# An AdaLN-conditioned FFN on one Trainium2 core: prologue order, six rows spread by DMA, borrowed buffers moved

## What is computed

```
att   = softmax(gelu(gelu(emb W0 + b0) W1 + b1) W2 + b2)          # 32 x 8, emb = cond_128
y[b]  = (sum_k att[b,k] weight[k]) x[b] + (att bias_k)[b]         # 128x128 by 128x2048, "conv"
yb    = bfloat16(y)
qg,sg = dynamic_quant(yb * inv_gate);  qu,su = dynamic_quant(yb * inv_up)   # codes -127..127, a scale a row
gate  = (qg w_gate^T) sg s_gate;       up = (qu w_up^T) su s_up            # 2048 -> 1024
inter = bfloat16(clip(silu(gate) up, -10, 10))
qi,si = dynamic_quant(inter * inv_inter)
out   = x + (qi w_down^T) si s_down                                # 1024 -> 2048
```

## Time and profile before

| | |
|---|---|
| median of the runs | 838.83 us (838.81 to 840.03) |
| profiled execution, its own time | 838.61 us |
| its span, first to last instruction | 836.8 us |
| PE busy | 811.7 us, 97% |
| DVE, ACT, GpSimd busy | 715.6, 443.0, 152.1 us |
| bytes moved by DMA | 117.72 MB |
| mean granted TensorE clock | 0.993 |

### The profile page before, as it was taken

The page is one execution under the profiler, slowest core; times in us unless marked ns, Lnnn a source line. Parts: engine busy times, 40 slices in busy tenths (PEclk is TensorE's granted clock), DMA queues, the critical chain, the costliest instruction groups (busy, mean ns, idle before and its releaser), DMA issues.

```text
span 836.8 us, 9194 instructions
## 1 busy us (share of the span) xinstructions
PE 811.7 (97%) x3531; PEld 365.9 (44%) x3531; DVE 715.6 (86%) x799; ACT 443.0 (53%) x379; POOL 152.1 (18%) x146
## 2 busy tenths in 40 slices
PE   7898969899999999999999999999999999999997
PEld 2344434344444444444444444444444444444443
DVE  5575847999888898888889988888898888889968
ACT  2767322566565555565555556555555565545541
POOL 5630002111222222012222210222221012222000
PEclk9999989999999999999999999999999999999999
DMA  9962534355445454444554544445454454554242
GB/s 272 216 149 51 101 101 169 104 159 160 113 151 164 139 164 139 117 140 120 164 160 142 141 136 139 113 151 163 139 162 141 119 132 127 164 157 145 89 113 101
DMA packets 157918, 117.72 MB, mean 141 GB/s; under 512 B 147497, under 2 KB 147625, under 8 KB 148274
## 3 DMA queue, kind: packets, MB, share of 16 engines
q1 hardware_dynamic: 156146, 104.55, 41.4%
q0 software_dynamic: 1728, 12.58, 7.5%
HBM read 59.44 MB, written 33.55 MB: 111 GB/s over the span
## 4 chain that ended last, share of the span: by engine, by line
PE 88%; DVE 6%; ACT 2%; DMA 2%; issue 1%; DVEq 0%; ACTq 0%
PE up_ps L506 24%; PE gate_ps L506 24%; PE down_ps L580 24%; PE conv_ps L453 13%; DVE amax L875 1%; DMA wd<-w_downT 1%; DMA qgT<-qg 1%; PE down_ps L423 1%; DVE region L965 1%; DVE region L971 1%; ACT qg L686 0%; PE up_ps L423 0%; DVE region L981 0%; PE gate_ps L580 0%; PE conv_ps L415 0%
## 5 line engine op out<-in xcount | busy, mean ns | idle before, releaser
L506 PE MATMUL gate_ps<-wg,qgT 128*128 128x512 bf16 x992 | 219.7, 379 | 1.6 <-ACT qgT L730 1.6
L580 PE MATMUL down_ps<-wd,qiT 128*128 128x512 bf16 x912 | 214.8, 379 | 2.1 <-ACT qiT L766 2.1
L506 PE MATMUL up_ps<-wu,quT 128*128 128x512 bf16 x960 | 216.7, 379 | 0.0
L875 DVE TENSOR_REDUCE amax<-region 128x1 f32<-128x2048 f32 (+1 forms) x93 | 178.8, 1923 | 1.3
L357 POOL TENSOR_TENSOR prod<-wexp,att_bc 128x1024 f32<-128x1024 f32 x31 | 58.9, 1901 | 541.6 <-DVE region L915 516.6
L506 PEld LDWEIGHTS gate_ps<-wg,qgT 128*128 128x128 bf16 x992 | 96.9, 98 | 119.4 <-ACT qgT L730 2.1
L580 PEld LDWEIGHTS down_ps<-wd,qiT 128*128 128x128 bf16 x912 | 89.1, 98 | 128.0 <-issue 30.0
L506 PEld LDWEIGHTS up_ps<-wu,quT 128*128 128x128 bf16 x960 | 93.8, 98 | 113.5 <-issue 0.6
L453 PE MATMUL conv_ps<-xt,aggw 128*128 128x512 f32 x256 | 124.7, 612 | 6.1 <-issue 2.9
L686 ACT ACTIVATE qg<-region,recip 128x2048 f16<-128x2048 f32 x30 | 60.1, 2002 | 125.9 <-DVE recip L885 125.9
L677 ACT ACTIVATE y<-conv_ps,aggb 128x512 bf16<-128x512 f32 x120 | 81.8, 686 | 75.4 <-PE conv_ps L453 70.7
(11 more groups left out here) (124 smaller groups left out, 509.3 us busy)
## 6 DMA issues: line engine op xcount, KB each, us to landing
xt<-x SPq DMA_DIRECT2D x32, 1024.0 KB, 4.8
out<-xt SPq DMA_DIRECT2D x31, 1024.0 KB, 4.0
wg<-w_gateT POOLq DMA_DIRECT2D x4, 1024.0 KB, 19.0
wu<-w_upT POOLq DMA_DIRECT2D x4, 1024.0 KB, 19.5
wd<-w_downT POOLq DMA_DIRECT2D x4, 1024.0 KB, 7.7
out<-xt SPq DMA_DIRECT2D x4, 256.0 KB, 2.7
wexp<-weightT SPq DMA_DIRECT2D x1, 512.0 KB, 3.8
qgT<-qg SPq DMA_TRANSPOSE x28, 3.7
```

What stands on the lines that cost most here:

```text
L506: last = nc.tensor.matmul(acc[:, n * BANK:(n + 1) * BANK], codes[:, k * P:(k + 1) * P], wts[:, k, n * BANK:(n + 1) * BANK], start=(k == 0) ...
L580: last = nc.tensor.matmul(down_bank(t, c), qiT_at(t)[:, k * P:(k + 1) * P], wd[:, k, c * BANK:(c + 1) * BANK], start=(k == 0), stop=(k == ...
L875: nc.vector.tensor_reduce(amax[:, i:i + 1], src, axis=AX.X, op=ALU.max, apply_absolute_value=True).then_inc(max_ready, 1)
```

## The change

- The six rows are arrays of their own. SyncE spreads each over all partitions by one DMA (`partition_broadcast(P)`), inv_gate behind x tile 0, inv_up and s_gate once w_gate's third quarter is in (`sp.wait_ge(wg_in[2], 16)`), s_up, inv_inter and s_down once its last is in. x tile 3 is sent behind them.
- PE's spread and warm products, ACT's spread_copy and GpSimd's partition_broadcast go. Those who waited for spread_out or row_spread wait for rows_in of the row.
- GpSimd's aggregate(1) waits for agg_step K, the end of aggregate(0) on DVE, instead of att_dve 7.
- GATE_HOME[1] is `prod` instead of part 5 of `wd`; QIT_HOME is in `qg` instead of `prod`. So gate_out(1) on DVE waits for agg_ready 4, turned_i(0) on ACT for the turning of qg(3) on PE, quant_g(4) on ACT for down_done 8, and GpSimd no longer waits for down_done 8 ahead of aggregate(5). Other waits that served the old homes go.
- Order on PE: turn_u(0) ahead of gate(2, h0) instead of behind it. On ACT: quant_g(1) ahead of conv_out(2); turned_g(2), quant_u(0), turned_u(0) and then silu(0); quant_g(3) ahead of silu(2); quant_u(3) behind turned_i(2). On DVE: quant_g(3) ahead of gate_out(2), and quant_u(3) behind inner(2).

The diff, cut to its core:

```diff
-        GATE_HOME = [down_sc2[:, :], wd_part(5, fp32), wd_part(6, fp32)]
+        GATE_HOME = [down_sc2[:, :], prod[:, :, :].rearrange("p k o -> p (k o)"), wd_part(6, fp32)]
...
-        prod_bf = prod[:, :, :].rearrange("p k o -> p (k o)").bitcast(bf16)
-        QIT_HOME = [prod_bf[:, 0:KI * P], prod_bf[:, KI * P:2 * KI * P]]
+        qg_bf = qg[:, :].bitcast(bf16)
+        QIT_HOME = [qg_bf[:, 0:KI * P], qg_bf[:, KI * P:2 * KI * P]]
...
 @block.sync
             sp.dma_start(mlp_s, mlp).then_inc(mlp_in, 16)
             sp.dma_start(b2_s, b2.partition_broadcast(P)).then_inc(b2_in, 16)
-            sp.dma_start(invg_s[0], rows[:, 0:I]).then_inc(rows_in[0], 16)
             sp.dma_start(wexp[:, :, :], weightT).then_inc(wexp_in, 16)
-            sp.dma_start(invg_s[1], rows[:, I:2 * I]).then_inc(rows_in[1], 16)
             sp.dma_start(xslot(0), x[0, :, :]).then_inc(x_in[0], 16)
+            sp.dma_start(invg_bc[:, :], inv_gate.partition_broadcast(P)).then_inc(rows_in[INVG], 16)
             sp.dma_start(xslot(1), x[1, :, :]).then_inc(x_in[1], 16)
-            for i, home in enumerate((invu_s[0], invu_s[1], swg_s)):
-                sp.dma_start(home, rows[:, (2 + i) * I:(3 + i) * I]).then_inc(rows_in[2 + i], 16)
             sp.dma_start(xslot(2), x[2, :, :]).then_inc(x_in[2], 16)
-            for i, home in enumerate((swu_s, invi_s, swd_s[0], swd_s[1])):
-                sp.dma_start(home, late_rows[:, i * I:(i + 1) * I]).then_inc(late_in[i], 16)
+            sp.wait_ge(wg_in[2], 16)
+            sp.dma_start(invu_bc[:, :], inv_up.partition_broadcast(P)).then_inc(rows_in[INVU], 16)
+            sp.dma_start(swg_bc[:, :], s_gate.partition_broadcast(P)).then_inc(rows_in[SWG], 16)
+            sp.wait_ge(wg_in[3], 16)
+            sp.dma_start(swu_bc[:, :], s_up.partition_broadcast(P)).then_inc(rows_in[SWU], 16)
+            sp.dma_start(invi_bc[:, :], inv_inter.partition_broadcast(P)).then_inc(rows_in[INVI], 16)
+            sp.dma_start(swd_bc[:, :], s_down.partition_broadcast(P)).then_inc(rows_in[SWD], 16)
             sp.wait_ge(gcodes_ready, 2)
             sp.dma_start(xslot(3), x[3, :, :]).then_inc(x_in[3], 16)
...
 @block.gpsimd
-            pool.wait_ge(att_dve, ATT - 1)
+            pool.wait_ge(agg_step, K)
             aggregate(1)
...
-            for i in range(4):
-                pool.wait_ge(late_in[i], 16)
-            spread(swu_bc[:, :], swu_s)
-            spread(invi_bc[:, :], invi_s)
-            spread(swd_bc[:, 0:I], swd_s[0])
-            spread(swd_bc[:, I:H], swd_s[1])
...
-            pool.wait_ge(row_spread, SWD)
             load(wd, w_downT, 2, wd_in)
             pool.wait_ge(prod_ready, 3)
             load(wd, w_downT, 3, wd_in)
-            pool.wait_ge(down_done, NC * 2)
...
 @block.tensor
-            pe.wait_ge(ones_set, 1)
-            warm(9)
             pe.wait_ge(mlp_in, 16)
+            pe.wait_ge(ones_set, 1)
             nc.tensor.matmul(hid_ps, w0_s, embT_s, start=True, stop=True).then_inc(hid_mm, 1)
-            warm(1)
...
-            warm(3)
...
-            for u in range(4):
-                spread(u)
-                warm(1)
             conv(0)
-            spread(4)
-            spread(5)
             conv(1)
             turn_g(0)
             conv(2)
             gate(0, HALVES[0])
-            spread(6)
-            spread(7)
             turn_g(1)
             gate(0, HALVES[1])
-            spread(8)
-            spread(9)
             gate(1, HALVES[0])
             turn_g(2)
             gate(1, HALVES[1])
+            turn_u(0)
             gate(2, HALVES[0])
-            turn_u(0)
             conv(3)
...
 @block.scalar, quant_g(t)
+                elif t == EARLY + 1:
+                    act.wait_ge(down_done, NC * 2)
 turned_u(t)
-                if t == 1:
-                    act.wait_ge(row_spread, SWD)
 turned_i(t)
                 if t == 0:
-                    act.wait_ge(agg_ready, 4)
+                    act.wait_ge(gturn_mm, GTURN["g", EARLY] + 2)
 order
-            for u in range(4):
-                spread_copy(u)
             conv_out(0)
-            spread_copy(4)
-            spread_copy(5)
             conv_out(1)
             quant_g_first()
             turned_g(0)
+            quant_g(1)
             conv_out(2)
-            quant_g(1)
-            spread_copy(6)
-            spread_copy(7)
             turned_g(1)
             quant_g(2)
-            spread_copy(8)
-            spread_copy(9)
+            turned_g(2)
             quant_u(0)
-            turned_g(2)
+            turned_u(0)
             silu(0)
-            turned_u(0)
             quant_u(1)
             conv_out(3)
             silu(1)
             turned_u(1)
             quant_u(2)
+            quant_g(3)
             silu(2)
-            quant_g(3)
             turned_u(2)
             quant_i(0)
-            quant_u(3)
             turned_g(3)
             turned_i(0)
             quant_i(1)
             turned_i(1)
             quant_i(2)
             turned_i(2)
+            quant_u(3)
             turned_u(3)
...
 @block.vector, gate_out(t)
-                if t == 2:
-                    dve.wait_ge(row_spread, SWD)
+                if t == 1:
+                    dve.wait_ge(agg_ready, 4)
 order
             quant_u(2)
+            quant_g(3)
             gate_out(2)
-            quant_g(3)
             inner(0)
-            quant_u(3)
             inner(1)
             inner(2)
+            quant_u(3)
```

More of the change, by code:

```diff
@@ L3, with adaln_ffn @@
 from contextlib import ExitStack
-def adaln_ffn(nc, x, mlp, b2, weightT, w_gateT, w_upT, w_downT, rows, late_rows, out):
+def adaln_ffn(nc, x, mlp, b2, weightT, w_gateT, w_upT, w_downT, inv_gate, inv_up, s_gate, s_up, inv_inter, s_down, out):
     fp32 = mybir.dt.float32
@@ L168, in adaln_ffn @@
         wexp_in = sem("wexp_in")
-        rows_in = [sem(f"rows_in{i}") for i in range(5)]
-        late_in = [sem(f"late_in{i}") for i in range(4)]
+        rows_in = [sem(f"rows_in{i}") for i in range(6)]
         x_in = [sem(f"x_in{i}") for i in range(XS)]
@@ L237, in adaln_ffn @@
         result_ready = sem("result_ready")
-        INVG, INVU, SWG = 4, 8, 10
-        SWU, INVI, SWD = 1, 2, 4
+        INVG, INVU, SWG, SWU, INVI, SWD = range(6)
         ATT = 8
@@ L250, in adaln_ffn @@
         last_turn_ps = [bank(up_ps, h).bitcast(fp16)[:, 0:BANK] for h in range(2)]
[L252 to L257, removed]
         def gate_acc(t):
@@ L365, in aggregate @@
                 nc.gpsimd.tensor_tensor(w, prod[:, 0, :], prod[:, 1, :], ALU.add).then_inc(agg_ready, 1)
-            def spread(dst, row):
-                nc.gpsimd.partition_broadcast(dst, row).then_inc(row_spread, 1)
             nc.gpsimd.memset(ident[:, :], 0.0).then_inc(ident_set, 1)
@@ L411, in _ @@
         def _(pe):
[L413 to L424, removed]
+            pe.wait_ge(mlp_in, 16)
             pe.wait_ge(ones_set, 1)
-            warm(9)
-            pe.wait_ge(mlp_in, 16)
             nc.tensor.matmul(hid_ps, w0_s, embT_s, start=True, stop=True).then_inc(hid_mm, 1)
-            warm(1)
             pe.wait_ge(hid_act, 1)
             nc.tensor.matmul(hid_ps, w1_s, h1, start=True, stop=True).then_inc(hid_mm, 1)
-            warm(3)
             pe.wait_ge(att_dve, 1)
@@ L444, in conv @@
                 for c in cs:
-                    if t == 0 and c < 2:
-                        pe.wait_ge(spread_out, 3)
-                    elif t == 3 and c < 2:
+                    if t == 3 and c < 2:
                         pe.wait_ge(uturn_out, c + 1)
@@ L450, in conv @@
                         pe.wait_ge(uturn_out, 9 + c)
-                    else:
+                    elif t > 0 or c >= 2:
                         pe.wait_ge(y_ready, NC * t + c - 1)
@@ L513, in gate @@
                         pe.wait_ge(qgT_ready, t - EARLY)
-                    if t == 0:
-                        pe.wait_ge(spread_out, INVG)
-                    elif t == 1:
-                        pe.wait_ge(spread_out, SWG)
-                    elif t == 2:
+                    if t == 2:
                         pe.wait_ge(gateval_ready, 1)
@@ L521, in gate @@
                         pe.wait_ge(upval_ready, 2)
-                    else:
+                    elif t > EARLY:
                         pe.wait_ge(gateval_ready, t)
@@ L659, in _ @@
         def _(act):
-            def spread_copy(u):
-                act.wait_ge(spread_mm, u + 1)
-                nc.scalar.activation(SPREAD_INTO[u], SPREAD_BANK[u], ACT.Copy).then_inc(spread_out, 1)
             def conv_out(t, cs=range(NC)):
@@ L890, in quant_g @@
                     dve.wait_ge(gcodes_ready, t - 1 if t == 2 else t)
-                elif t == 1:
-                    dve.wait_ge(spread_out, INVG)
                 if t == EARLY + 1:
@@ L902, in quant_u @@
                 if t == 0:
-                    dve.wait_ge(spread_out, INVU)
+                    dve.wait_ge(rows_in[INVU], 16)
```

(21 more changed lines are left out.)

12 lines of the change are left out of this document (removed).

## The result

The changed kernel takes 844.46 us (median of 6 runs, 843.02 to 848.72) against 838.82 before; the ratio is 1.0072, 95% interval 1.0053 to 1.0091. That is 5.6 us or 0.7% slower; the forecast was 846.0.

A forecast was written before the change was run, and what follows sets the result against it. PE's entry into its steady part, from about 180 us, was taken to fix the time. 3.4 + 0.9 - 1.2 + 2.5 + 1.6 = +7.2 on 838.61 gave 845.8, 846.0 as a median; range 836 to 852.

The forecast's parts named there:

- conv(3) starts: PE's conv(3) waits for x tile 3 and starts at 68.5 instead of 65.06: +3.4 us.
- conv(3) at the lower clock: After some 10 us of PE idle, conv(3) runs at 1.2 GHz at first, 5.97 us instead of 5.1: +0.9.
- chain to the last quarter: With quant_u(3) behind inner(2) on DVE, the chain to the last down weights' issue gets shorter: -1.2 us.
- quant_u(3) at turn_u(3): PE waits for ACT's later quant_u(3), so down(1) starts 4.1 instead of 1.6 us behind turn_i(2): +2.5.
- clock behind it: PE's 3.1 us idle at turn_u(3) lowers the clock afterwards, costing 0 to 2 us, middle case +1.6.
- x tile 3: Load queued behind the rows on SyncE's queue, sharing engines with down weights 0: lands at 68.5, between 67 and 70.5.
- The rows ahead of it: Broadcasts on SyncE's queue end at 41, 46.5, 52, 57.7, 64.6; beside weights 6.9 us per 1 MB, 5.6 per 0.5 MB.
- The start: Aggregate(0) steps at 497 ns, conv(0) near 13.9, 5.1 us earlier; 4 us given back, PE ready for conv(3) near 58.
- Rival 1: Hidden rows, faster: x tile 3 is there when PE arrives at 58; 833 to 834.6 us, chance 17%.
- Rival 3: Slow broadcasts: 128 reads of one row run slower than a tile; 857 at half speed, above 850: chance 12%.

The follow-up runs named there:

- e2: The changed kernel with x tile 3 sent behind inv_up and s_gate, ahead of s_up, inv_inter and s_down: 832.64 us, ratio to before 0.9921.
- f1: The changed kernel with GpSimd's aggregate(3) waiting until DVE's product of quant_g(1) is done: 847.62 us, ratio to before 1.0106.
- f3: The changed kernel with GpSimd's aggregate(1) waiting for att_dve 7 again, as before the change: 844.49 us, ratio to before 1.0062.
- e1: The changed kernel with quant_u(3) ahead of turned_i(2) on ACT: 841.74 us, ratio to before 1.0038, runs in two groups.
- f2: The changed kernel with aggregate(3) behind DVE's product of quant_g(1), and down weights 0 sent only once x tile 3 has landed: 844.20 us, ratio to before 1.0059.
- e3: The changed kernel with quant_u(3) ahead of turned_i(2) on ACT and x tile 3 ahead of the late rows: 829.98 us, ratio to before 0.9880.
- e4: The kernel before with one edit, GpSimd's aggregate(1) waiting for the end of DVE's aggregate(0): 836.55 us, ratio to before 0.9971.
- g1: The changed kernel with ACT's quant_u(3) swap, x tile 3 ahead of late rows, aggregate(3) behind DVE's product, conv_out(2) ahead of quant_g(1): 827.75 us, ratio to before 0.9866.
- g3: g1 with sixteen unread products of 512 columns on PE ahead of its wait for the last quarter of the down weights: 826.48 us, ratio to before 0.9853.

## Why the prediction was right, step by step

The starts of the same work in the two profiled runs give the account; each size is the growth of the lag since the line before. The rows of after that it uses and that were not shown:

```profile
99.34 0.61 PE L410 MATMUL down_ps<-ident,qi 128*128 128x128 f16 x8
...
121.09 0.61 PE L410 MATMUL conv_ps<-ident,qi 128*128 128x128 f16 x8
...
126.01 8.34 PE L527 MATMUL down_ps<-wd,qg 128*128 128x512 bf16 x32
...
134.19 3.62 PE L457 MATMUL up_ps<-wu,quT 128*128 128x512 bf16 x16
...
155.07 3.63 PE L457 MATMUL gate_ps<-wg,qgT 128*128 128x512 bf16 x16 [1.49 <-ACT qgT L664]
```

| step | forecast | measured | from |
|---|---|---|---|
| conv(3) starts | +3.4 | +2.0 | 67.04 - 65.06 |
| conv(3) at the lower clock | +0.9 | +0.3 | turn_i(0): 99.34 against 97.02 is +2.3 in all |
| chain to the last quarter | -1.2 | -1.3 | its issue: 105.15 against 104.12, +1.0 in all |
| its landing | 0 | -0.3 | 112.71 against 112.00, +0.7 in all |
| clock at down(0) | 0 | +0.9 | turn_i(2): 121.09 against 119.50, +1.6 in all |
| quant_u(3) at turn_u(3) | +2.5 | +2.7 | down(1): 126.01 against 121.68, +4.3 in all |
| clock behind it | +1.6 | +1.3 | up(3): 134.19 against 128.58, +5.6 in all |
| sum | +7.2 | +5.6 | span: +5.5; gate(4) at 155.07 against 149.58 |

- **x tile 3** was the right mechanism, shown by e2: without its late place the same kernel is 11.8 us quicker. It was sized 1.5 us too late (68.5). I had down weights 0 go at 62 and share its last part. They went at 64.87 since the held product of quant_g(1) had made the prologue 5 us slower, and x tile 3 was all but through (their first packets run at 66). In f1 they went at 59.78, and it took until 71.9, later than my upper end of 70.5. So the range of that term was too narrow, and its cause is a race that I had not looked for. The forecast of 846.0 lies between what the two outcomes of the race give, 844.5 and 847.6 (f1), without my having known of it; that part is luck. The changed kernel's own 848.72 is probably a run with the quick start.
- **The rows ahead of it** came later than told, and their errors cancel. They landed at 42.6, 49.9, 56.1, 62.3 and 64.6, where I had 41, 46.5, 52, 57.7 and 64.6: a 0.5 MB row took 6.2 to 7.3 us beside weights instead of 5.6, but the weights ended near 61 instead of 64 to 65, and s_down's 1 MB took 2.3 us instead of 6.9.
- **conv(3)** took 5.6 us, but the 5.1 that I compared it with were not full clock alone. A conv without waits takes 3.87 us (137.64), and conv(3) before held a wait of 1.33 us for ACT besides. So the lower clock cost about 1.7 us, and the wait that it covered gave 1.3 back.
- **The start** came as told: 352 ns a step, conv(0) at 13.19, and no gain at the end (f3). The 4 us that I gave back for contention cover what happened: PE was ready at 59.5 where I had 58, and at 54.2 in e1, where DVE's product was not held.
- **turn_u(3)** came with its size, 3.0 us of idle and its clock (e1: 2.8 and 1.2).
- **The chain to the down weights** got 1.3 shorter, by quant_i(1) waiting for turned_i(0), as worked out. The clock at down(0) was not in the sum. The idle of 5.7 us before had cost it a part already, and after 117 to 121.2 is still at 0.84. This 0.9 us is no effect of the change: behind an idle of 3.9 to 4.2 us the same 26 products took 7.15 us in f2, 7.47 in e1 and f1 and 8.66 in e2. The profiled execution drew a long one.
- **Rival 1** (faster) is what e2 and e3 made of the kernel: its 833 to 834.6 were met by 832.64, by freeing x tile 3 from the queue, not by the weights' yielding. Its condition did not hold in the change itself. **Rival 3** (slow broadcasts) is refuted by the 0.86 MB in 2 us.
- What stays open: why GpSimd's product, which by the record starts 0.90 to 1.34 us behind DVE's, holds it all the same. In e4 even a DVE operation of 0.68 us that began at 23.92, 1.29 us ahead of that product, ended only at 27.71. e1's lower group was not profiled either; that DVE's product was held there and x tile 3 came at 67 is inferred from f1 and f2.

## What to carry to other kernels

In a queue that works in order, a load's place is its due time: sort the queue by when each piece is first waited for, and look at who else will use the engines then. The six broadcasts are not what made the kernel slower: e2 and e3 carry them and are 6 to 9 us faster than the kernel before (what the broadcasts alone cost, no run shows). x tile 3 behind rows of which the first is needed some 17 us after it (75.87 against 58.36 in e2) cost 9 to 12. When work moves on one engine, walk PE's order again and look for a step whose input now comes two operations later; a swap of two lines on ACT gave back 4 us at its place and 2.7 at the end (e2 to e3).

## What I had not expected of the hardware

- A product of 2.3 us on DVE takes 5.0 to 5.4 beside GpSimd or 2.3, and starts 0.17 us apart, counted from GpSimd's descriptors, lie on either side (0.16 in e1, 0.33 in e2). That race most likely split the 12 runs of e1 into two groups 5 us apart, with the quicker start in the slower group.
- An idle of PE can cost more than its own length: behind 3.00 us without any product down(1) took 8.13 us, behind 0.7 us 6.91. Sixteen products that nobody reads, in 4 us of idle, kept the clock at 1.00, but the next wait, for DVE, took nearly all of it back: 0.24 us were left in the traces of g1 and g3.
- The two queues take turns row by row, whatever a row's size: 114 to 113 packets with 8 KB rows, 125 to 128 with 4 KB rows. Halving the row halves the queue's bytes for the same turns.
